# Two softmax maps of a second attention layer joined by GpSimd before their transposes, quads unrolled

## The chip, the cores and the metric

The kernel runs on one core of a Trainium2 chip. The metric is the device time of one launch in microseconds (us), as the median of the runs shown. The profile is of one execution.

## The reference, cut to what matters

A two-layer transformer tower over 32 images of 37 tokens, width 192, 12 heads of 16. The layer-1 attention is the part that changes:

```python
q = (x @ Wq).reshape(B, N, 2, H, D).transpose(2, 0, 3, 1, 4)   # two sets of queries
k = (x @ Wk).reshape(B, N, 2, H, D).transpose(2, 0, 3, 1, 4)   # and of keys
v = (x @ Wv).reshape(B, N, H, D).transpose(0, 2, 1, 3)
out = softmax(q[0] k[0]^T / 4) v - exp(lambda_p) * softmax(q[1] k[1]^T / 4) v
h = layernorm(h + out @ Wo + bo)
```

Before it stand a patch embedding, a layer-0 attention and a mixture of 64 slots (its output is combined and normalized here, as h); behind it an expert layer with top-4 gates and a last norm.

## The kernel before, in words

Every engine has one queue of instructions written by hand, and semaphores order them: TensorE (pe), VectorE (dve), ScalarE (act), GpSimd (pool) and the DMA queue (sp). One stage follows the other: layer 0 (to 231 us), the slots' matmuls, bound by the weights' DMA (to 423 us), the stage that changes (`l1_pe`, `l1_dve`, `l1_act`, `l1_pool`, L867 to L1026, 423 to 634 us), the top-4 gates (to 718 us), the expert units (to 977 us), and the last norm.

The 32 images are 16 pairs, two images in partitions 0 to 36 and 64 to 100 (101 rows, `ROWS`). Four pairs are a quad, and there are four quads. `steps` (L861) writes out quads 0 and 3 and makes quads 1 and 2 a loop. In a quad (`step`, L889):

- `combine` (L868) makes the slots' output of a pair (L871), VectorE adds h1 (L926) and takes the norm's moments (`ln_moments`, L571, L574), GpSimd makes the reciprocal root (`pool_rstd`, L584, L586), and VectorE scales (`ln_scale`, L579) into `h_in`.
- `pe_turn` transposes `h_in` (L334), `take_turned` copies it (L344). `pe_qk` (L353) makes queries and keys in blocks of 96 rows, two for each map: 16 products of 296 columns. ScalarE copies queries (L442), and ScalarE (L447) and VectorE (L457) write each key block six times, masked for one head each. `pe_v` (L370) makes the values, `dve_v` (L474) takes them.
- `pe_attention` (L420) goes over 8 units, a pair and a map each. A unit's scores (L388) are 444 columns in one bank; VectorE takes the maximum and subtracts it (L480, L485), ScalarE takes the exponential (L490), TensorE makes 6 transposes (L399), ScalarE copies them (L497), TensorE mixes with the values and a column of ones (L415, 12 small products), and `dve_norm` (L520 to L533) divides by the row sums, weights the second map with lambda and subtracts it. TensorE's queue runs two units ahead of the mixing.
- `pe_turn_rows` (L552), `take_rows` (L560), the projection (L905), the residual (L961), its moments, GpSimd's root, `ln_scale`, the transposes for the expert layer (L880, L979), and GpSimd's `h3_all` (L1011).

Map 0 of the next quad's queries and keys is made at the end of a quad, map 1 only after the residual. At the start GpSimd also writes ones into `zs` (L1020), which waits only for the first root:

```python
pool.wait_ge(L0["rstd"], QUADS + 1)
pool.memset(zs[6 * SR:ZR, :, :], 1.0).then_inc(s_set, 1)
```

## Time and profile before

| what | value |
|---|---|
| median of 3 runs | 1006.28 us (1004.51 to 1006.57) |
| the profiled execution, its own time | 1001.23 us |
| its span | 999.4 us |
| granted TensorE clock, mean | 0.854 |
| TensorE, VectorE, ScalarE, GpSimd busy | 794.8, 562.6, 368.2, 106.6 us |

Busy time is that of the whole span, over stages with different limits; a stage is read from its own windows and its own timeline. A line of a timeline can hold several instructions (x6), and its duration is then from the first start to the last end. A bracket says how long the engine had been idle, and what ended that.

### The profile page before, as it was taken

Reading aid. Unit: us, or ns where it says so; the run is one execution under the profiler, and the core shown is the slowest. Engines: PE = TensorE matmul, PEld = TensorE weight load, DVE = VectorE, ACT = ScalarE, POOL = GpSimd, SP = SyncE. Lnnn points to the kernel's source line nnn. Section 1 sums busy time; section 2 is a strip of 40 time slices with the busy share of each in tenths; the row PEclk is TensorE's granted clock in tenths of the full one; section 3 lists DMA queues with packets and bytes.
Section 4 is the critical chain, followed back from the end, with each engine's and each line's share of the span. In section 5 each row is a group of like instructions: output and inputs, shape, how many; then the busy total and the mean of one; then the engine's idle time right before and its main releaser. Section 6 shows DMA issues by size and latency. Waiting matters only on the chain.

```text
span 999.4 us, 19725 instructions
## 1 busy us (share of the span) xinstructions
PE 794.8 (80%) x6898; PEld 452.0 (45%) x6898; DVE 562.6 (56%) x1562; ACT 368.2 (37%) x785; POOL 106.6 (11%) x134
## 2 busy tenths in 40 slices
PE   6889899839888687529988988634399989989992
PEld 4567676635434343216766666311133333333331
DVE  4565664640110111155686859588687858848785
ACT  0313221303211210004333444143387767758770
POOL 0020202022121200030010010132200000000002
PEclk9898987957976979758798979855599999989996
DMA  8510100003999999993000000362300000000001
GB/s 301 225 38 1 36 0 0 1 1 139 416 424 424 415 414 427 279 123 45 1 2 1 0 1 2 121 73 49 86 13 2 2 2 1 0 2 1 0 1 38
DMA packets 25016, 102.56 MB, mean 103 GB/s; under 512 B 3552, under 2 KB 14756, under 8 KB 20724
## 3 DMA queue, kind: packets, MB, share of 16 engines
q1 hardware_dynamic: 23894, 98.37, 29.2%
q0 software_dynamic: 1056, 3.44, 0.9%
q8 instruction: 27, 0.44, 0.2%
q14 instruction: 39, 0.31, 0.1%
HBM read 93.08 MB, written 5.07 MB: 98 GB/s over the span
## 4 chain that ended last, share of the span: by engine, by line
PE 60%; DVE 17%; DMA 11%; issue 6%; POOL 2%; ACT 2%; DVEq 0%; POOLq 0%; SPq 0%; ACTq 0%
DMA stream<-in_fc_dram 10%; PE P L1461 8%; PE P L1436 7%; PE P L1445 7%; PE P L353 6%; PE P L769 3%; PE P L388 3%; PE P L415 3%; PE P L370 2%; PE P L399 2%; DVE work L579 2%; PE P L1454 2%; PE P L738 2%; PE P L744 2%; PE P L1179 2%
## 5 line engine op out<-in xcount | busy, mean ns | idle before, releaser
L1603 DVE TENSOR_TENSOR work<-work,P 128x396 f32<-128x396 f32 x384 | 193.1, 562 | 65.1 <-PE P L1445 45.0
L1532 ACT ACTIVATE work<-P 128x396 f32<-128x396 f32 x384 | 178.6, 500 | 56.9 <-PE P L1436 55.8
L1436 PE MATMUL P<-stream 99*128 x384 | 129.5, 340 | 12.3 <-ACT work L1532 10.5
L1445 PE MATMUL P<-early,middle 96*128 x384 | 129.8, 339 | 0.6 <-DVE work L1603 0.6
L1461 PE MATMUL P<-work 128*32 128x396 f32 x768 | 84.6, 508 | 0.0
L1436 PEld LDWEIGHTS P<-stream 99*128 99x128 bf16 x384 | 37.7, 98 | 100.6 <-ACT work L1532 54.2
L584 POOL TENSOR_SCALAR work<-work 101x4 f32<-101x4 f32 x16 | 3.7, 230 | 652.8 <-DVE work L574 652.8
L796 ACT ACTIVATE work<-P 128x768 f32<-128x768 f32 x16 | 13.0, 812 | 153.8 <-PE P L751 153.8
L811 DVE COPY work<-P 128x768 f32<-128x768 f32 x16 | 15.3, 958 | 96.0 <-PE P L759 96.0
L490 ACT ACTIVATE work<-work 101x444 f32<-101x444 f32 x48 | 28.1, 585 | 85.9 <-DVE work L485 85.9
L1106 PE MATMUL P<-early 128*37 128x192 f32 x384 | 47.8, 337 | 10.1 <-DMA early<-in_patches_dram 7.1
L1445 PEld LDWEIGHTS P<-early,middle 96*128 96x128 bf16 x384 | 37.8, 98 | 35.3 <-DVE work L1603 17.4
L816 DVE COPY work<-P 128x192 f32<-128x192 f32 x16 | 5.7, 358 | 79.0 <-PE P L769 79.0
L769 PE MATMUL P<-stream,work 128*32 128x192 f32 x768 | 46.0, 403 | 3.2 <-DVE work L811 3.2
L415 PE MATMUL P<-work 101*37 101x34 f32 x1152 | 46.0, 209 | 2.8 <-DVE work L474 2.8
L399 PE MATMUL P<-ident,work 101*128 101x101 f32 x288 | 36.3, 264 | 12.6 <-ACT work L490 10.6
L415 PEld LDWEIGHTS P<-work 101*37 101x37 f32 x1152 | 41.5, 123 | 8.1 <-issue 3.9
L1106 PEld LDWEIGHTS P<-early 128*37 128x37 f32 x384 | 34.4, 117 | 22.4 <-issue 10.4
L353 PE MATMUL P<-work,stream 96*96 96x296 f32 x128 | 41.3, 487 | 4.1 <-DVE work L961 3.5
L480 DVE TENSOR_REDUCE work<-P 101x12 f32<-101x444 f32 x48 | 29.6, 616 | 22.5 <-PE P L388 22.2
L457 DVE TENSOR_SCALAR stream<-P,hmask 96x296 f32<-96x296 f32 x48 | 21.5, 515 | 36.8 <-PE P L353 36.8
L399 PEld LDWEIGHTS P<-ident,work 101*128 101x128 f32 x288 | 27.4, 144 | 29.7 <-ACT work L490 19.4
(212 smaller groups left out, 1247.6 us busy)
## 6 DMA issues: line engine op xcount, KB each, us to landing
stream<-in_fc_dram SPq DMA_DIRECT2D x16, 2304.0 KB
stream<-in_fc_dram SPq DMA_DIRECT2D x16, 1536.0 KB, 17.5
stream<-in_fc_dram SPq DMA_DIRECT2D x16, 768.0 KB, 19.1
early<-stream SPq DMA_DIRECT2D x36, 99.0 KB, 2.3
early<-in_patches_dram SPq DMA_DIRECT2D x4, 888.0 KB, 5.1
stream<-w_dram SPq DMA_DIRECT2D x6, 512.0 KB
work<-in_w_dram SPq DMA_DIRECT2D x1, 2048.0 KB, 8.3
stream<-z_dram SPq DMA_DIRECT2D x6, 297.0 KB, 10.3
```

The costliest lines, as they stand in the source:

```text
L353: mm = pe.matmul(P[0:FH, at + mc, 0:QT], w[:, kc, m * D + mc * FH:m * D + (mc + 1) * FH], h_t[:, kc, :, :], start=(kc == 0), stop=(kc == 1))
L388: mm = pe.matmul(P[64 * e:64 * e + T, u % 2, mc * HH * T:(mc + 1) * HH * T], q_t[:, m, mc, b * T:(b + 1) * T], k_heads[:, m, mc, b, :, :], ...
L399: mm = pe.transpose(P[:, 4 + 2 * (u % 2) + hp // 3, (hp % 3) * ROWS:(hp % 3 + 1) * ROWS], probs[0:ROWS, u % 2, hp, :, :].rearrange("p a k ...
L415: mm = pe.matmul(P[64 * e:64 * e + T, 2 + u % 2, hp * w2:(hp + 1) * w2], probs_t[0:ROWS, u % 2, hp, 64 * e:64 * e + T], v_blk[0:ROWS, 2 * ...
L480: dve.tensor_reduce(row_max[0:ROWS, u % 2, :], src, AX, ALU.max).then_inc(L["row_max"], 1)
L769: mm = pe.matmul(P[32 * j:32 * j + B, 6 + u, 0:D], hidden_t[:, u, c, B * j:B * (j + 1)], fc2[:, u, c, j, :], start=False, stop=(c == HC - ...
L1106: mm = pe.matmul(P[64 * e:64 * e + T, 2 + j // 2, (j % 2) * D:(j % 2 + 1) * D], patches[:, c, 2 * j + e, :], w_patch[:, c, :], start=(c == ...
L1436: pe.matmul(P[:, n % 3, 0:TC], w1s[:, seg, i * 128:(i + 1) * 128], zs[:, seg, ds(it * TC, TC)], start=True, stop=True).then_inc(s_u1, 1)
L1445: pe.matmul(P[:, 3 + n % 3, 0:TC], gate_sel[:, c, :], ws[:, 2 * seg + hh, ds(it * TC, TC)], start=True, stop=True).then_inc(s_bc, 1)
L1461: pe.matmul(P[32 * j:32 * j + 32, 6 + sq, 0:TC], w2[:, i, seg, :], gated[:, n % 8, :], start=False, stop=(hh == 1 and c == CH // 2 - 1), s ...
L1532: act.activation(act_out[:, n % 4, :], P[:, n % 3, 0:TC], ACT.Gelu_apprx_tanh).then_inc(s_ua, 1)
L1603: dve.tensor_tensor(gated[:, n % 8, :], act_out[:, n % 4, :], P[:, 3 + n % 3, 0:TC], ALU.mult).then_inc(s_ug, 1)
```

## The change

It touches only the stage of layer 1, and where its four weight matrices lie and are loaded. All four quads are written out. Queries and keys come in three blocks of 128 rows (8 heads; the middle block holds 4 heads of each map), 12 products of 296 columns, and a key block is written eight times: blocks 0 and 2 by ScalarE, block 1 by VectorE. A step is now a pair with both maps: its scores fill two banks (888 columns), VectorE takes maximum, difference, sums and reciprocals over 24 head rows, ScalarE the exponential in place, and GpSimd multiplies both maps with their weights (`differ`) and subtracts them. One set of 6 transposes and 12 mixing products follows, without the column of ones, and ScalarE copies the result (`take_mixed`). The residual's norm goes to GpSimd (`normed`), with h plus bias (`with_bias`). The parts of neighbouring quads are put between the pairs. The memset of `zs` now waits for `with_bias(0)`.

```diff
-k_heads1 = tenant(stream, FH, 12 * D, [2, 2, QB, HH, T])
+k_heads1 = tenant(stream, 128, 0, [3, QB, 8, T])
...
-late = Tenants(stream)
+late = Tenants(early)
...
+exps = [shifted, w([128, 2, NH, T])]
+res = w([128, QP, D])
...
+hb = rowc[:, 0:QP, :]
+q_t1 = tenant(work, 128, shared + 2 * QB * H_STRIDE, [3, QT])
...
+    sp.wait_ge(s_emb, QP * QUADS)
+    sp.wait_ge(s_prep_misc, PREP_MISC)
+    for dst, name in ((w_q1, "w_q1"), (w_k1, "w_k1"), (w_v1, "w_v1"), (w_o1, "w_o1")):
+        sp.dma_start(dst, io[name]).then_inc(s_late, 16)
...
-    for dst, name in ((w_q1, "w_q1"), (w_k1, "w_k1"), (w_v1, "w_v1"), (w_o1, "w_o1")):
-        sp.dma_start(dst, io[name]).then_inc(s_late, 16)
...
+    def combine(q):
+        if q:
+            pe.wait_ge(L1["taken"], QP * (q - 1) + 1)
         for j in range(QP):
...
+            mm = pe.matmul(P[0:ROWS, 4 + j // 2, (j % 2) * D:(j % 2 + 1) * D], combine_all[:, q * QP + j, :],
+                           y2[:, q * QP + j, :], start=True, stop=True, skip_group_check=True)
...
+    def turn_in(q):
+        if q:
+            pe.wait_ge(L1["taken"], QP * (q - 1) + 2)
...
+    def turn_x3(q):
+        pe.wait_ge(L1["shifted"], min(QP * (q + 1) + 2, QP * QUADS))
...
+    def qk(q, n):
+        if n == 0:
+            pe.wait_ge(L1["h_t"], QP * (q + 1))
+        if n < 2 and q:
+            pe.wait_ge(L1["shifted"], QP * q - 1 + n)
+        if n == 2:
+            pe.wait_ge(L1["q_ready"], 3 * q + 1)
+            pe.wait_ge(L1["k_ready_a"], 2 * HB * q + HB)
+        for w, bank, made in ((w_q1, 2 * (n % 2), "q_made"), (w_k1, 2 * (n % 2) + 1, "k_made")):
             for kc in range(2):
...
+                mm = pe.matmul(P[:, bank, 0:QT], w[:, kc, n * 128:(n + 1) * 128], h_t[:, kc, :, 0:T],
+                               start=(kc == 0), stop=(kc == 1))
...
+    def scores(q, p):
+        g = QP * q + p
+        if p == 0:
+            pe.wait_ge(L1["q_ready"], 3 * (q + 1))
+            pe.wait_ge(L1["k_ready_a"], 2 * HB * (q + 1))
+            pe.wait_ge(L1["k_ready_v"], HB * (q + 1))
+        if p >= 2:
+            pe.wait_ge(L1["shifted"], g - 1)
+        if p == 3 and q:
+            pe.wait_ge(LO["h_t"], QP + QP * q)
+        for m in range(2):
+            for e in range(2):
+                b = 2 * p + e
+                for n, h, to, at in ((2 * m, 0, HB, 4 * T * m), (1, 4 * m, 4 * m + 4, HB * T * (1 - m))):
+                    mm = pe.matmul(P[64 * e:64 * e + T, 2 * (g % 2) + m, at:at + (to - h) * T],
+                                   q_t1[:, n, b * T:(b + 1) * T], k_heads1[:, n, b, h:to, :],
+                                   start=True, stop=True, skip_group_check=True)
...
+    def turn_probs(q, p):
+        g = QP * q + p
+        if g >= 2:
+            pe.wait_ge(L1["taken"], g - 1)
+        if p == 0:
+            pe.wait_ge(L1["v_ready"], 4 * (q + 1))
+        elif p == 1 and q:
+            pe.wait_ge(LO["resid"], QP * q)
+        elif p == 2 and q + 1 < QUADS:
+            pe.wait_ge(L0["resid"], QP * (QUADS + q + 2))
+        elif p == 3 and q + 1 < QUADS:
+            pe.wait_ge(L1["h_t"], QP * (q + 2))
+        elif p == 1:
+            pe.wait_ge(L1["h_t"], QP)
+        pe.wait_ge(L1["mapped"], g + 1)
...
+    combine(0)
+    turn_in(0)
+    for n in range(3):
+        qk(0, n)
+    values(0)
+    for q in range(QUADS):
+        more = q + 1 < QUADS
+        scores(q, 0)
+        scores(q, 1)
+        if q:
+            project(q - 1)
+        scores(q, 2)
+        turn_probs(q, 0)
+        mix(q, 0)
+        turn_probs(q, 1)
+        if more:
+            combine(q + 1)
+        if q:
+            turn_x3(q - 1)
+        scores(q, 3)
+        mix(q, 1)
+        turn_probs(q, 2)
+        if more:
+            turn_in(q + 1)
+        mix(q, 2)
+        if more:
+            qk(q + 1, 0)
+        turn_probs(q, 3)
+        if more:
+            qk(q + 1, 1)
+        mix(q, 3)
+        if more:
+            values(q + 1)
+            qk(q + 1, 2)
+        turn_attn(q)
+    project(QUADS - 1)
     turn_x3(QUADS - 1)
...
+    def softmax(q, p):
+        g = QP * q + p
+        src = P[0:ROWS, 2 * (g % 2):2 * (g % 2) + 2, 0:NH * T].rearrange("p m (h k) -> p m h k", k=T)
+        dve.wait_ge(L1["scores"], g + 1)
+        dve.tensor_reduce(row_max1[0:ROWS, g % 2, :, :], src, AX, ALU.max).then_inc(L1["row_max"], 1)
+        dve.wait_ge(L1["row_max"], g + 1)
+        if g >= 2:
+            dve.wait_ge(L1["mapped"], g - 1)
+        dve.tensor_tensor(exps[g % 2][0:ROWS], src, spread(row_max1[0:ROWS, g % 2, :, :], 3, T),
+                          ALU.subtract).then_inc(L1["shifted"], 1)
+    def weights(q, p):
+        g = QP * q + p
+        dve.wait_ge(L1["exps"], g + 1)
+        dve.tensor_reduce(sums[0:ROWS, g % 2, :, :], exps[g % 2][0:ROWS], AX, ALU.add).then_inc(L1["sums"], 1)
+        dve.wait_ge(L1["sums"], 3 * g + 1)
+        dve.reciprocal(shares[0:ROWS, g % 2, :, :], sums[0:ROWS, g % 2, :, :]).then_inc(L1["sums"], 1)
+        dve.wait_ge(L1["sums"], 3 * g + 2)
+        dve.tensor_tensor(shares[0:ROWS, g % 2, 1, :], shares[0:ROWS, g % 2, 1, :], lam[0:ROWS, :],
+                          ALU.mult).then_inc(L1["sums"], 1)
...
+    def residual(q):
+        dve.wait_ge(s_hb, q + 1)
+        if q:
+            dve.wait_ge(LO["h_out"], QP * q)
...
+    combined(0)
+    normed(0)
+    take_in(0)
+    dve.wait_ge(s_hm, 1)
+    keys(0, 1)
+    values(0)
+    for q in range(QUADS):
+        more = q + 1 < QUADS
+        softmax(q, 0)
+        weights(q, 0)
+        softmax(q, 1)
+        if q:
+            residual(q - 1)
+        weights(q, 1)
+        softmax(q, 2)
+        if more:
+            combined(q + 1)
+        if q:
+            take_out(q - 1)
+        weights(q, 2)
+        if more:
+            normed(q + 1)
+        softmax(q, 3)
+        if more:
+            take_in(q + 1)
+        weights(q, 3)
+        if more:
+            keys(q + 1, 1)
+            values(q + 1)
+    residual(QUADS - 1)
...
+    take_in(0)
+    act.wait_ge(s_hm, 1)
+    queries(0, 0)
+    keys(0, 0)
+    queries(0, 1)
+    queries(0, 2)
+    keys(0, 2)
+    for q in range(QUADS):
+        more = q + 1 < QUADS
+        exp(q, 0)
+        exp(q, 1)
+        take_probs(q, 0)
+        exp(q, 2)
+        take_mixed(q, 0)
+        take_probs(q, 1)
+        if q:
+            take_out(q - 1)
+        exp(q, 3)
+        take_mixed(q, 1)
+        take_probs(q, 2)
+        if more:
+            take_in(q + 1)
+        take_mixed(q, 2)
+        if more:
+            queries(q + 1, 0)
+            keys(q + 1, 0)
+        take_probs(q, 3)
+        if more:
+            queries(q + 1, 1)
+        take_mixed(q, 3)
+        if more:
+            queries(q + 1, 2)
+            keys(q + 1, 2)
+        take_rows(act, q, s_at, s_att, 6)
+    take_out(QUADS - 1)
...
+    def differ(q, p):
+        g = QP * q + p
+        pool.wait_ge(L1["sums"], 3 * (g + 1))
+        pool.tensor_tensor(exps[g % 2][0:ROWS], exps[g % 2][0:ROWS], spread(shares[0:ROWS, g % 2, :, :], 3, T),
+                           ALU.mult).then_inc(L1["weighted"], 1)
+        pool.wait_ge(L1["weighted"], g + 1)
+        if g >= 2:
+            pool.wait_ge(L1["probs_turned"], g - 1)
+        e = exps[g % 2][0:ROWS].rearrange("p m (h a) k -> p m h a k", a=2)
+        pool.tensor_tensor(probs[0:ROWS, g % 2, :, :, 0:T], e[:, 0], e[:, 1], ALU.subtract).then_inc(L1["mapped"], 1)
...
+    def normed(q):
+        settle(pool, LO["mv"], QP * q + QP)
+        pool.tensor_scalar(var_o[0:ROWS, :], mv_o[0:ROWS, :, 1], EPS, None, ALU.add).then_inc(LO["var"], 1)
+        pool.wait_ge(LO["var"], q + 1)
+        pool.tensor_tensor(rstd_o[0:ROWS, :], var_o[0:ROWS, :], negh[0:ROWS, :], ALU.pow).then_inc(LO["rstd"], 1)
+        pool.wait_ge(LO["rstd"], q + 1)
+        if q:
+            pool.wait_ge(LO["h_turned"], 2 * q)
+        for j in range(QP):
+            pool.tensor_scalar(h_out[0:ROWS, j, :], res[0:ROWS, j, :], mv_o[0:ROWS, j, 0:1],
+                               rstd_o[0:ROWS, j:j + 1], ALU.subtract, ALU.mult).then_inc(LO["h_out"], 1)
...
+    with_bias(0)
     pool.wait_ge(s_fo, GROUPS)
-    pool.wait_ge(L0["rstd"], QUADS + 1)
+    pool.wait_ge(s_hb, 1)
     pool.memset(zs[6 * SR:ZR, :, :], 1.0).then_inc(s_set, 1)
     pool.wait_ge(s_set, 1)
-    steps(pool, step)
+    for q in range(QUADS):
+        differ(q, 0)
+        if q:
+            normed(q - 1)
+        differ(q, 1)
+        if q:
+            keep(q - 1)
+            with_bias(q)
+        if q + 1 < QUADS:
+            pool_rstd(pool, L0, QUADS + q + 1)
+        differ(q, 2)
+        differ(q, 3)
+    normed(QUADS - 1)
+    keep(QUADS - 1)
...
```

## Rows read from the trace of the kernel before

**Rows 1.** Windows: engines' busy time in one quad; first line names the columns.

```profile
core 0: us, PE busy (x) PEld busy (x) DVE busy (x) ACT busy (x) POOL busy (x), PEclk, DMA share, GB/s
498.00:543.00 45.00, 40.14 (x449) 29.99 (x448) 33.51 (x99) 17.40 (x38) 4.82 (x6) 0.92 0.01 1
```

**Rows 2.** Timeline (start us, us, engine, line): scores of quads 0, 2, 3; end.

```profile
462.77 1.52 PE L388 MATMUL P<-stream,work 96*37 96x222 f32 x14
...
554.17 0.96 PE L388 MATMUL P<-stream,work 96*37 96x222 f32 x8
...
600.95 0.95 PE L388 MATMUL P<-stream,work 96*37 96x222 f32 x8
...
633.42 0.53 DVE L979 COPY early<-P 96x148 f32<-96x148 f32 x2 [0.71 <-PE P L880]
```

**Rows 3.** Timeline at the start of the stage.

```profile
431.46 3.06 PE L871 MATMUL P<-early 128*101 128x192 f32 x8 [8.19 <-issue]
...
437.90 9.38 DVE L579 TENSOR_SCALAR work<-work 101x192 f32<-101x192 f32 x4 [1.62 <-POOL work L586]
437.99 8.01 POOL L1020 MEMSET stream<- 3x9504 bf16 x1
```

**Rows 4.** Timeline of quad 2: one instance of each TensorE piece.

```profile
547.08 4.22 PE L353 MATMUL P<-work,stream 96*96 96x296 f32 x16 [1.19 <-DVE work L961]
...
551.23 2.87 PE L370 MATMUL P<-stream,work 96*37 96x96 f32 x64
...
559.08 0.74 PE L399 MATMUL P<-ident,work 101*128 101x101 f32 x6
...
563.43 0.93 PE L415 MATMUL P<-work 101*37 101x34 f32 x24
```

**Rows 5.** The same timeline: one instance of each VectorE piece.

```profile
545.93 1.01 DVE L961 TENSOR_TENSOR work<-P,work 101x384 f32<-101x384 f32 x2
...
553.95 1.23 DVE L579 TENSOR_SCALAR work<-work 101x192 f32<-101x192 f32 x4
...
562.57 0.23 DVE L522 RECIPROCAL work<-work 101x12 f32<-101x12 f32 x1
...
563.11 0.61 DVE L480 TENSOR_REDUCE work<-P 101x12 f32<-101x444 f32 x1
...
563.75 0.62 DVE L485 TENSOR_TENSOR work<-P,work 101x444 f32<-101x444 f32 x1
...
565.74 0.17 DVE L525 TENSOR_TENSOR work<-work,lam 101x12 f32<-101x12 f32 x1
...
576.90 0.95 DVE L942 TENSOR_TENSOR work<-work,rowc 101x768 f32<-101x768 f32 x1
```

**Rows 6.** The same timeline: ScalarE's and GpSimd's pieces.

```profile
548.83 1.04 POOL L586 TENSOR_TENSOR work<-work,negh 101x4 f32<-101x4 f32 x1
...
550.34 2.48 ACT L447 ACTIVATE stream<-P,hmask 96x296 f32<-96x296 f32 x6 [0.58 <-PE P L353]
...
555.37 1.81 POOL L1011 TENSOR_TENSOR h_all<-work,rowc 101x768 f32 x1 [5.50 <-DVE work L579]
...
564.41 0.59 ACT L490 ACTIVATE work<-work 101x444 f32<-101x444 f32 x1 [1.53 <-DVE work L485]
...
564.89 0.65 ACT L497 ACTIVATE work<-P 128x606 f32<-128x606 f32 x1
```

**Rows 7.** Timeline after the stage: small VectorE product alone, then beside GpSimd.

```profile
660.73 0.18 DVE L1571 TENSOR_TENSOR work<-work 128x32 f32<-128x32 f32 x1
...
663.74 1.06 POOL L1612 TENSOR_TENSOR work<-work 128x512 f32<-128x512 f32 x1 [1.91 <-DVE work L1567]
663.78 1.06 DVE L1571 TENSOR_TENSOR work<-work 128x32 f32<-128x32 f32 x1
```

**Rows 8.** Timeline before quad 1: TensorE at its lower clock.

```profile
485.58 1.27 PE L399 MATMUL P<-ident,work 101*128 101x101 f32 x6 [1.66 <-ACT work L490]
...
492.01 6.03 PE L353 MATMUL P<-work,stream 96*96 96x296 f32 x16
```

More of the change, by code:

```diff
@@ L316, in tower @@
         s_yt = sem("s_slot_inputs_taken")
-        s_keep = sem("s_h1_kept")
         SMALL_LOADS = [
@@ L975, in take_x3 @@
-        def take_x3(eng, copy, quad, g):
-            eng.wait_ge(LO["h_turned"], nth(quad, 2, g + 1))
-            src = P[0:FH, 4 + g, :].rearrange("p (j k e r) -> p j k e r", j=2, k=2, e=2)
-            for j in range(2):
-                copy(x3_t[:, :, ds(quad * QB + (4 * g + 2 * j), 2), :], src[:, j, :, :, 0:T]).then_inc(LO["h_t"], 1)
-        def l1_act(act):
-            def step(it, first, last):
-                act_q(act, L1, it, 2, (1,), None, k_heads1)
-                act_attention(act, L1, it, 2, None if first else lambda: take_x3(act, act.copy, it - 1, 0))
-                if not last:
-                    take_turned(act, act.copy, L1, it + 1, 0, h_t)
-                take_rows(act, it, s_at, s_att, 6)
-                if not last:
-                    act_q(act, L1, it + 1, 2, (0,), None, k_heads1)
-            act.activation(lam[:, :], lam[:, :], ACT.Exp).then_inc(s_lam, 1)
-            take_turned(act, act.copy, L1, 0, 0, h_t)
-            act_q(act, L1, 0, 2, (0,), None, k_heads1)
-            steps(act, step)
-            take_x3(act, act.copy, QUADS - 1, 0)
@@ L997, in l1_pool @@
-        def l1_pool(pool):
-            def stage(quad):
-                pool.tensor_copy(comb_r[:, :, :], combine_all[:, ds(quad * QP, QP), :]).then_inc(s_cr, 1)
-            def step(it, first, last):
-                if not last:
-                    pool.wait_ge(s_mix, nth(it, QP, QP))
-                    stage(it + 1)
-                    pool_rstd(pool, L0, it + (QUADS + 1))
-                pool_rstd(pool, LO, it)
-                pool.wait_ge(LO["h_out"], nth(it, QP, QP))
-                pool.tensor_tensor(h3_all[0:ROWS, ds(it * QP, QP), :], h_out[0:ROWS, :, :],
-                                   spread(rowc[0:ROWS, 5, :], 1, QP), ALU.add).then_inc(s_h3, 1)
+            combine(0)
@@ new lines, in l1_pe, with take_h, take_x3 @@
+            project(QUADS - 1)
+            turn_x3(QUADS - 1)
+        def take_h(copy, q, g):
+            src = P[0:FH, 6 + g, :].rearrange("p (j k e r) -> p j k e r", j=2, k=2, e=2)
+            for j in range(2):
+                copy(h_t[:, :, 4 * g + 2 * j:4 * g + 2 * j + 2, 0:T], src[:, j, :, :, 0:T]).then_inc(L1["h_t"], 1)
+        def take_x3(copy, q, g):
+            src = P[0:FH, 2 + g, :].rearrange("p (j k e r) -> p j k e r", j=2, k=2, e=2)
+            for j in range(2):
+                at = q * QB + 4 * g + 2 * j
+                copy(x3_t[:, :, at:at + 2, :], src[:, j, :, :, 0:T]).then_inc(LO["h_t"], 1)
```

265 lines of the change are left out of this document (170 added, 95 removed).

## The prediction

> **What bounds the kernel now.** I read the busy slices first: the stage of layer 1 is the only one the change touches. Its windows come next: in a middle quad TensorE is busy 40 of 45 us, VectorE 33.5, GpSimd 5 [rows 1]. Then the timeline for the quads' beginnings: first scores at 462.8, 554.2 and 600.9, the end at 634.0 [rows 2]. So quads 0 and 1 together take 91.4, quad 2 takes 46.8, quad 3 has nothing to prepare and takes 33.0: 171.1 in all. Inside a quad, eight units follow one another every 2.9 us while two are in flight, and some 20 us go to the handover, where TensorE and VectorE take turns. At the start one thing stands out: four scalings that take 1.23 elsewhere [rows 5] take 9.38 beside GpSimd's memset of 8.0 [rows 3].
>
> **Durations, each for one step.** TensorE [rows 4]: scores of a pair 1.9 (the same 1776 columns as two units of 0.96 [rows 2]); transposes 0.75; mixing 0.9; a block's queries and keys, 8 instructions of L353, 2.1; values 2.9; combine of four pairs 1.8 (at most the 3.1 of [rows 3], which has waits in it); eight transposes 1.5, the nearest row being L399's six in 0.74 to 1.27 [rows 4, 8].
>
> VectorE [rows 5]: 444 columns take 0.61 and 768 take 0.95, so 888 take 1.07: maximum and subtraction together 2.2; sums 1.07, reciprocal of 24 (12 take 0.23) 0.3, lambda 0.17: weights 1.6. Residual or combine's sum, 1.0, and its moments 1.4: 2.4 (GpSimd's root starts at 548.83, 2.9 after L961, with 0.5 of its own ahead). Scaling 1.25. A pair of copies 0.55.
>
> ScalarE [rows 6]: exponential of 888 between 0.59 (444 columns) and twice that; 0.95, since a part is fixed. Copy of transposes 0.65, mixed result 0.35 (estimate), a key block 8 x 0.41 = 3.3.
>
> GpSimd has no such product in the trace. 512 elements take 1.06 [rows 7], 768 take 1.81 [rows 6]. The bounds for 888 are 1.06 and 2.1; it has more elements than either row, so I take 1.95, and 1.0 for the difference of 444. With 0.3 to be released, a map step takes 3.25; from 1.9 to 3.5 is possible. The residual's norm: root 1.6 (1.04 is the power [rows 6]) and four scalings of 192 at about 0.4: 3.3.
>
> The Trainium skill's GPSIMD Engine Reference (Engine selection) advises against just this: elementwise work with two inputs is put at about twice VectorE's time. By that the product would take 2.15 and the difference 1.25, and the sum below would be some 3.5 us longer. My sum goes by the rows, which are GpSimd's own.
>
> **A middle quad after the change**, from the issue of its first scores. Scores 1.9, maximum and subtraction to 4.15, exponential to 5.15, weights to 6.8, second softmax to 9.05, residual of the quad before to 11.65, second weights to 13.3. GpSimd finished map 0 at 10.15, but takes the residual's norm before map 1: 11.65 to 14.9. Map 1 is ready at 18.1. TensorE has mixed pair 0 by 12.6 and its next instruction is the transpose of map 1: it stands for 5.5 us, with combine, the old quad's transposes and the last scores queued behind. Then transposes 18.9, combine 20.7, VectorE's half sum and moments to 22.7 (it had been idle since 15.5), copy and third weights to 24.9. Scaling 26.2, last softmax 28.4, exponential 29.4, copy of pair 1's result (behind it in ScalarE's queue) 29.8, transposes of h 31.3, copies 31.9, and only now the last weights, 33.5. Map 3 is ready at 36.8, transposed 37.6, block 1's products 39.7, mixing 40.7, values 43.5, block 2's products 45.6, ScalarE's eight key copies 49.0. Period **49.0**, against 46.8.
>
> The other two by the same walk. Quad 0 has no residual, norm or h3 in it: map 1 at 15.15, combine's sum 19.9, third weights 21.5, last weights 30.2, map 3 33.6, next scores at **45.7**. Quad 3 prepares nothing, but its tail is serial: last weights at 27.2, map 3 30.6, transposes, copy, mixing, copy 33.4, transposes of rows 34.8, projection's start 35, residual to 40.4, norm on GpSimd 43.6, transposes and copies **44.6** (33.0 before). Together 45.7 + 2 x 49.0 + 44.6 = 188.3, against 171.1: +17.2.
>
> **The start.** The memset now follows the scalings: they take 1.25, not 9.38, -8.1. From there to the first scores I count 14.9 in place of 15.5 (8 fewer instructions of L353, but block 2 waits for ScalarE's block 0, then 3.3 of key copies): -8.8 in all. The memset runs beside products and copies out of PSUM and is over 5 us before the first scores; the first map step comes 7 us later. If that cover were gone it would cost up to 8.
>
> **Shared access.** A VectorE product of 0.18 took 1.06 beside a GpSimd product of 1.06, and a scaling waited 8 us for the memset [rows 7, 3]. Here `normed(q+1)`, four scalings out of SBUF, starts 0.2 before GpSimd's map 2. One scaling gets through; the others wait for the product, perhaps the difference: 2.1 to 3.1. I take 2.5 in each of three quads: +7.5. The lambda products fall where GpSimd is idle or in short steps: 0, or 2 each if they don't.
>
> **The clock.** After a sparse stretch TensorE was at its lower level: six transposes took 1.27 for 0.74, and sixteen of L353 6.03 for 4.22 although it worked without a break [rows 8, 4]. An idle of 5.5 us in each quad invites that. On the path of a middle quad: two sets of transposes +1.0, combine +0.5, block 1 +0.9, mixing and scores +0.6: +3.0; for quads 0 and 3 +2.0. In all **+10**, between 0 and 27 (the lower level for the whole path: 6 to 7 a quad).
>
> **At nothing:** the weights' four loads go ahead of the slots' stream, past nothing that runs; before, they were issued behind its last load. The staging copy of combine and the column of ones were beside other work. Writing out the loop: quads in it and outside it took alike. Merged semaphores change no order.
>
> **Sum:** +17.2 - 8.8 + 7.5 + 10 = +26, less 1 for the pieces where a lower clock and a blocked scaling overlap: +25. The profiled execution took 1001.2, 5 below the median of 1006.3; the stage is all of the change, so I put the +25 on the median: **1031**.
>
> **Rivals.**
> - *Bare waits* (0.13). Neither sharing nor clock costs: VectorE's scalings slip through before GpSimd asks, and products back to back keep the clock up. +8.4: 1015.
> - *GpSimd is quick* (0.20, the other side). If a map step takes 2.0, as its copies would suggest, map 1 comes 1.25 sooner and the norm's scalings 1.0, map 3 1.25, and the two waits in between shorten: 4.4 in quads 1 to 3, 2.5 in quad 0, 15.7 in all, and TensorE's idle shrinks to 3 us; at best neither clock nor sharing then costs anything. +8.4 - 15.7 = -7: 999. It decides from a map step under 2.6. For it: engine work in a middle quad is only some 32 on TensorE and 29 on VectorE, so there is room below 46 down to 985. Against it: 512 elements already take 1.06 [rows 7], and 768 take 1.81 [rows 6].
> - *The lower clock stays* (0.12). TensorE's work falls from 40 [rows 1] to 32 in 50 us, in bursts. +8.4 + 7.5 + 27: 1049.
> - *Ends meet* (0.05): errors of both signs cancel at 1006.
>
> **Numbers.** The forecast, 1018 to 1043, has 0.50. About 0.2% is what a measurement of this kernel can tell from no change. Faster comes from the quick GpSimd alone: 0.20. Same: 0.05. Slower: the rest, 0.75. The range of 8 in 10 goes from 1003, leaving out most of the quick case, to 1046, leaving out most of the slow clock.
>
> **What would show it.** Right: first scores near 454; quads near 48, 54, 54, 48 apart; a wait of TensorE's transposes for GpSimd's difference of 2 to 6 us once a quad; VectorE waiting for combine some 4 us; one `ln_scale` instruction of 2 us a quad; a product on GpSimd of 1.9 to 2.1; mean clock in the stage under 0.8. Wrong: a product under 1.3, quads under 44, or TensorE without such gaps.

## The result, and the profile after

The changed kernel takes **1046.96 us** in the median of four runs (1040.55, 1042.09, 1051.84, 1053.09) against 1006.42 for the kernel before. The ratio of the two means is 1.0382, 95% interval 1.0279 to 1.0485. The runs of either kernel fall into two groups some 11 us apart (before: 1001 to 1008 and 1014 to 1023), and this median lies between the two. The profiled execution is the fastest of the four, 1040.55 for a span of 1038.7; the one of before took 1001.2.

The page of the changed kernel, its first and second part in extract:

```profile
span 1038.7 us, 18375 instructions
...
PE 789.4 (76%) x6386; PEld 450.8 (43%) x6386; DVE 533.5 (51%) x1407; ACT 364.4 (35%) x781; POOL 172.2 (17%) x182
```

Three engines have less work than before, and GpSimd, with 66 us more, is busy 17% of the span: no engine became the bound, and yet the span is longer. Where the quads begin and end, from the timeline of TensorE and of VectorE (start, us, engine, line; L883 is combine, L959 the scores, L1068 the last copy of the turned rows):

```profile
436.04 2.85 PE L883 MATMUL P<-early,combine_all 128*101 128x192 f32 x8 [8.23 <-DMA early<-y_dram]
...
458.65 1.58 PE L959 MATMUL P<-stream,work 128*37 128x296 f32 x14 [0.64 <-issue]
...
507.74 4.66 PE L959 MATMUL P<-stream,work 128*37 128x296 f32 x32 [2.74 <-issue]
...
563.78 3.21 PE L959 MATMUL P<-stream,work 128*37 128x296 f32 x32 [2.74 <-issue]
...
618.35 3.21 PE L959 MATMUL P<-stream,work 128*37 128x296 f32 x32 [2.74 <-issue]
...
671.61 0.53 DVE L1068 COPY early<-P 96x148 f32<-96x148 f32 x2 [6.30 <-PE P L891]
```

And the windows from scores to scores (us, then the busy time of TensorE, its weight loads, VectorE, ScalarE and GpSimd, then the granted clock, the DMA share and GB/s):

```profile
458.65:507.74 49.09, 32.01 (x296) 24.75 (x297) 27.13 (x49) 15.57 (x34) 12.47 (x10) 0.79 0.10 13
507.74:563.78 56.04, 37.37 (x321) 28.73 (x322) 29.14 (x60) 16.68 (x38) 21.30 (x18) 0.73 0.01 1
563.78:618.35 54.57, 35.92 (x320) 28.14 (x321) 29.14 (x60) 16.67 (x38) 21.29 (x18) 0.75 0.00 1
618.35:672.14 53.79, 31.07 (x240) 23.78 (x240) 20.32 (x45) 9.97 (x20) 26.32 (x23) 0.61 0.00 1
```

From the first combine to the first scores it is 22.6 us, 31.3 before [rows 2, 3]. The four quads take 213.5, 171.1 before. The stage is 236.1 against 202.5: +33.6. Of the +39.3 between the two profiled executions, 4.6 lie ahead of the stage and 1.1 behind it, where the code is that of before.

One wait shows how a quad got long. Quad 1, the timeline of GpSimd, TensorE and VectorE (L1270 product, L1277 difference, L1289 the residual's scalings, L983 transposes of the maps, L883 the next quad's combine):

```profile
517.61 1.13 POOL L1277 TENSOR_TENSOR work<-work 101x444 f32<-101x444 f32 x1
...
521.83 3.99 POOL L1289 TENSOR_SCALAR work<-early 101x192 f32<-101x192 f32 x4
525.79 1.67 POOL L1270 TENSOR_TENSOR early<-early 101x888 f32<-101x888 f32 x1
527.54 1.12 POOL L1277 TENSOR_TENSOR work<-early 101x444 f32<-101x444 f32 x1
...
528.81 1.25 PE L983 MATMUL P<-ident,work 101*128 101x101 f32 x6 [7.35 <-POOL work L1277]
529.85 2.77 PE L883 MATMUL P<-early,combine_all 128*101 128x192 f32 x8
...
531.48 0.56 DVE L1103 TENSOR_TENSOR work<-P,h_all 101x384 f32<-101x384 f32 x1 [7.68 <-PE P L883]
```

The weights of map 1 (the map of the quad's second pair; pairs count from 0) were there at 521.7. GpSimd was on the residual's norm until 525.8, TensorE stood 7.35 us, and VectorE 7.68 us for a combine that needed nothing from map 1. The table of waits adds them up over the stage (us in all, times, longest):

```profile
PE P L983 <- POOL work L1277: 42.3, 12, 7.4
DVE work L1103 <- PE P L883: 31.0, 8, 9.3
```

The next quad's four scalings on VectorE (L589), beside GpSimd's product of map 2:

```profile
536.51 3.52 DVE L589 TENSOR_SCALAR work<-work 101x192 f32<-101x192 f32 x4
536.67 1.75 POOL L1270 TENSOR_TENSOR work<-work,early 101x888 f32<-101x888 f32 x1 [0.47 <-DVE early L1095]
```

GpSimd's rows of the stage, against which the prediction's estimates stand, and VectorE's scalings (the groups by form; busy us, mean ns):

```profile
L1289 POOL TENSOR_SCALAR work<-early 101x192 f32<-101x192 f32 x16 | 15.9, 1006 | 0.4
...
L1270 POOL TENSOR_TENSOR early<-early 101x888 f32<-101x888 f32 x8 | 13.4, 1676 | 28.4 <-DVE early L1095 28.4
L1277 POOL TENSOR_TENSOR work<-work 101x444 f32<-101x444 f32 x8 | 9.0, 1125 | 0.6
...
L589 DVE TENSOR_SCALAR work<-work 101x192 f32<-101x192 f32 x16 | 11.8, 796 | 1.9 <-POOL work L596 1.9
```

### The profile page after: what moved, and what is told of

Read it like the earlier page. It is cut to its first block, busy times and chain, and to the rows that moved or that the text cites. A ratio compares the mean times of both kernels' runs of the same rounds, so it can differ in the third digit from the quotient of the medians.

```text
span 1038.7 us, 18375 instructions
## 1 busy us (share of the span) xinstructions
PE 789.4 (76%) x6386; PEld 450.8 (43%) x6386; DVE 533.5 (51%) x1407; ACT 364.4 (35%) x781; POOL 172.2 (17%) x182
## 4 chain that ended last, share of the span: by engine, by line
PE 55%; DVE 17%; DMA 10%; issue 7%; POOL 6%; ACT 4%; POOLq 0%; SPq 0%; DVEq 0%; ACTq 0%
DMA stream<-in_fc_dram 9%; PE P L1765 8%; PE P L1740 7%; PE P L1749 7%; PE P L782 3%; PE P L925 2%; PE P L363 2%; DVE work L589 2%; PE P L1483 2%; PE P L1758 2%; DVE work L1880 2%; PE P L751 2%; POOL work L1289 2%; PE P L398 1%; PE P L757 1%
## 5 line engine op out<-in xcount | busy, mean ns | idle before, releaser
L782 PE MATMUL P<-stream,work 128*32 128x192 f32 x768 | 48.2, 417 | 3.2 <-DVE work L824 3.2
L983 PE MATMUL P<-ident,work 101*128 101x101 f32 x96 | 16.6, 332 | 42.3 <-POOL work L1277 42.3
L1410 PEld LDWEIGHTS P<-early 128*37 128x37 f32 x384 | 34.6, 118 | 22.8 <-issue 10.5
L959 PE MATMUL P<-stream,work 128*37 128x296 f32 (+1 forms) x256 | 32.3, 407 | 12.9 <-issue 8.9
L1715 PE MATMUL P<-ident,work 128*128 128x128 f32 x40 | 11.2, 434 | 36.5 <-DVE work L1894 36.5
L925 PE MATMUL P<-work,early 96*128 96x296 f32 x96 | 35.8, 532 | 2.1 <-ACT stream L1225 1.5
L782 PEld LDWEIGHTS P<-stream,work 128*32 128x32 f32 x768 | 28.7, 136 | 19.4 <-DVE work L824 5.0
L777 PE MATMUL P<-fc_b,slot_sel 4*128 4x192 f32 x32 | 11.5, 445 | 30.3 <-DMA stream<-in_fc_dram 30.3
L983 PEld LDWEIGHTS P<-ident,work 101*128 101x128 f32 x96 | 13.3, 191 | 45.7 <-issue 45.3
L751 PE MATMUL P<-stream,slot_sel 4*128 4x384 f32 x64 | 31.2, 615 | 0.0
```

What stands on the lines that cost most here:

```text
L751: pe.matmul(P[:, 2 * u + n, 0:HID // 2], slot_sel[:, :], fc1_b[:, u, n * (HID // 2):(n + 1) * (HID // 2)], start=True, stop=False, skip_gr ...
L782: mm = pe.matmul(P[32 * j:32 * j + B, 6 + u, 0:D], hidden_t[:, u, c, B * j:B * (j + 1)], fc2[:, u, c, j, :], start=False, stop=(c == HC - ...
L925: mm = pe.matmul(P[:, bank, 0:QT], w[:, kc, n * 128:(n + 1) * 128], h_t[:, kc, :, 0:T], start=(kc == 0), stop=(kc == 1))
L959: mm = pe.matmul(P[64 * e:64 * e + T, 2 * (g % 2) + m, at:at + (to - h) * T], q_t1[:, n, b * T:(b + 1) * T], k_heads1[:, n, b, h:to, :], s ...
L983: mm = pe.transpose(P[:, pair_bank(g) + hp // 3, (hp % 3) * ROWS:(hp % 3 + 1) * ROWS], probs[0:ROWS, g % 2, hp, :, :].rearrange("p a k -> ...
L1410: mm = pe.matmul(P[64 * e:64 * e + T, 2 + j // 2, (j % 2) * D:(j % 2 + 1) * D], patches[:, c, 2 * j + e, :], w_patch[:, c, :], start=(c == ...
```

## The experiments

Twelve kernels, each with one profiled execution; two were timed in five rounds. Times in us; q0 to q3 are the periods from the first scores of a quad to those of the next (q3: to the last copy of the turned rows), stage is from the first combine to that copy. "Time" is that of the profiled execution.

| kernel | first combine | to scores | q0 | q1 | q2 | q3 | stage | time |
|---|---|---|---|---|---|---|---|---|
| before | 431.5 | 31.3 | 91.4 for both | | 46.8 | 33.0 | 202.5 | 1001.2 |
| after | 436.0 | 22.6 | 49.1 | 56.0 | 54.6 | 53.8 | 236.1 | 1040.6 |
| e1 | 436.9 | 22.7 | 49.2 | 53.2 | 54.6 | 53.7 | 233.4 | 1036.9 |
| e2 | 440.2 | 23.4 | 48.5 | 52.0 | 53.0 | 53.7 | 230.6 | 1039.2 |
| e3 | 437.5 | 22.7 | 47.7 | 54.5 | 54.6 | 55.1 | 234.6 | 1040.5 |
| e6 | 448.9 | 22.6 | 49.1 | 51.7 | 52.1 | 46.4 | 221.8 | 1036.8 |
| e5 | 438.7 | 22.5 | 49.0 | 53.9 | 54.2 | 54.1 | 233.7 | 1039.5 |
| e7 | 448.2 | 22.5 | 49.0 | 56.0 | 54.6 | 53.8 | 235.9 | 1052.5 |
| b1 | 437.0 | 23.3 | 91.4 for both | | 46.8 | 33.0 | 194.6 | 998.8 |
| x1 | 437.1 | 22.7 | 37.9 | 38.6 | 46.7 | 42.9 | 188.8 | 992.7 |
| x2 | 437.0 | 22.8 | 32.6 | 34.2 | 34.1 | 42.9 | 166.6 | 972.1 |
| x3 | 436.5 | 23.0 | 39.3 | 39.6 | 40.6 | 47.3 | 189.7 | 992.5 |
| x4 | 437.1 | 22.8 | 41.2 | 40.9 | 41.0 | 43.4 | 189.3 | 993.8 |
| x5 | 431.2 | 23.0 | 32.6 | 34.2 | 34.0 | 43.1 | 166.9 | 966.8 |

**One part of these periods is no edit's.** The first scores of a quad take 3.21 us at the upper level of TensorE's clock and 4.6 or more where they begin at the lower one, behind the same idle time of 2.74. In the changed kernel q1 has the one and q2 the other, and the first transposes come 11.15 and 9.68 us after the first scores:

```profile
518.89 0.71 PE L983 MATMUL P<-ident,work 101*128 101x101 f32 x6 [2.05 <-POOL work L1277]
...
573.46 0.71 PE L983 MATMUL P<-ident,work 101*128 101x101 f32 x6 [2.04 <-POOL work L1277]
```

That is the whole difference between q1 and q2. In the experiments on the changed kernel it falls on other quads. e1, q2:

```profile
561.96 4.64 PE L959 MATMUL P<-stream,work 128*37 128x296 f32 x32 [2.75 <-issue]
...
573.07 0.71 PE L983 MATMUL P<-ident,work 101*128 101x101 f32 x6 [2.04 <-POOL work L1277]
```

So here are the periods less what the first transposes came later than 9.68 us (9.74 in q0), called "at equal first scores" below:

| kernel | q0 | q1 | q2 | q3 | four quads against the changed kernel |
|---|---|---|---|---|---|
| after | 49.1 | 54.6 | 54.6 | 53.8 | |
| e1 | 49.2 | 53.2 | 53.2 | 52.3 | -4.3 |
| e2 | 48.5 | 51.5 | 51.6 | 53.7 | -6.7 |
| e3 | 47.7 | 53.0 | 53.1 | 53.6 | -4.6 |
| e6 | 49.1 | 50.2 | 50.6 | 46.4 | -15.8 |
| e5 | 49.0 | 52.5 | 52.8 | 53.2 | -4.6 |
| e7 | 49.0 | 54.6 | 54.6 | 53.8 | -0.1 |

**e1: map 1 ahead of the residual's norm** (GpSimd's queue)

```diff
     differ(q, 0)
+    differ(q, 1)
     if q:
         normed(q - 1)
-    differ(q, 1)
```

> GpSimd makes pair 1's maps before it takes the residual's norm; nothing else moves. In the changed kernel the norm stands 5.3 us ahead of them (root 1.3, four scalings 1.0 each) in quads 1 to 3. Theory 'a serial chain of hand-overs': the wait of TensorE's transposes for pair 1's maps falls from 7.4 to about 3.4 us, but the old quad's h_out, GpSimd's two additions and the next root then come later, so that a middle quad gains only 1 to 2 us and quad 3 about 3: stage 236 -> 230. Rival 'the transposes' wait is what counts': 4 us in each of three quads, stage 224. Rival 'other work hides it': no change.

The stage falls by 2.7. At equal first scores it is 1.4 to 1.5 in each of the three quads that the edit touches, 4.3 in all, near the 1 to 2 of the theory (3 were expected in q3). TensorE's wait for map 1 falls from 7.4 to 3.3, but the norm now comes later, and with it the old quad's transposes ahead of the last scores; the wait for map 2 rises from 0.8 to 2.8 in q1 and q2. The next wait in the row takes most of it.

**e2: combine ahead of the transposes of map 1** (TensorE's queue)

```diff
+    if more:
+        combine(q + 1)
     turn_probs(q, 1)
-    if more:
-        combine(q + 1)
```

> TensorE's queue: combine(q+1) goes ahead of the transposes of pair 1. VectorE waits 7.7 us for it in a middle quad. Theory 'queue order': that wait goes, but the transposes for the expert layer and the copies still stand behind pair 1's maps, so the third weights come 2.5 to 3 us sooner: about 7 us over quads 0 to 2, stage 229. Rival 'GpSimd's maps end everything': no change (within 1 us). Rival 'the whole wait of VectorE returns': 18 to 20 us.

-5.5, and at equal first scores -6.7: 0.6 in q0, 3.1 in q1 and 2.9 in q2, as the theory had it (2.5 to 3 in each of three quads), but for q0. VectorE starts on the next quad's moments sooner, but its norm is still behind the third weights.

**e3: the next quad's norm alone, not beside the product**

```diff
     if q + 1 < QUADS:
         pool_rstd(pool, L0, QUADS + q + 1)
+        pool.wait_ge(L0["h_out"], QP * (QUADS + q + 2))
     differ(q, 2)
```

> GpSimd waits for the four scalings of normed(q+1) before it starts the product of map 2, so that the two don't run at once. In the changed kernel the scalings take 3.5 us instead of 1.25. Theory 'shared access': the last softmax comes 2.3 us sooner in quads 0 to 2, stage 236 -> 229; GpSimd's third maps come 1.2 later, which TensorE covers. Rival 'GpSimd's delay counts': gain under 3 us in all, or a loss of up to 3.

The four scalings take 1.25 again in every quad, so the 2.3 us of shared access are real (VectorE's longest single one is 0.38, 1.74 in the changed kernel):

```profile
536.74 1.25 DVE L589 TENSOR_SCALAR work<-work 101x192 f32<-101x192 f32 x4
...
538.07 1.68 POOL L1270 TENSOR_TENSOR work<-work,early 101x888 f32<-101x888 f32 x1 [1.64 <-DVE work L589]
```

The stage falls by 1.5 only. At equal first scores q0, q1 and q2 lose 1.4 to 1.6 each, 4.6 with a little in q3; the first scores of q2 and q3, at the lower level in this execution (4.77 and 4.79 for 3.21), took 3.0 of that back. So some 1.5 of the 2.3 lie on the path, with GpSimd's map 2 coming later by the edit itself.

**e6: the residual's four scalings back on VectorE**, behind the third softmax

```diff
-    for j in range(QP):
-        pool.tensor_scalar(h_out[0:ROWS, j, :], res[0:ROWS, j, :], mv_o[0:ROWS, j, 0:1],
-                           rstd_o[0:ROWS, j:j + 1], ALU.subtract, ALU.mult).then_inc(LO["h_out"], 1)
...
     softmax(q, 2)
+    if q:
+        scaled(q - 1)
```

> The residual's four scalings (4 x 1.0 us on GpSimd) go to VectorE (1.25 in all), behind its third softmax; the root stays on GpSimd. Theory 'the scalings are the mis-sized term': pair 1's maps come 4 us sooner in quads 1 to 3, and after the last quad another 2.7: stage 236 -> about 222. Rival 'VectorE pays it back': 4 us at the end of quad 3 only, stage 232.

The last quad's scalings go to VectorE too. -14.3, as expected; at equal first scores -15.8: 4.3, 4.0 and 7.4 in q1 to q3, most in q3, where the norm stands once ahead of map 1 and once in the serial tail. No other single edit to the changed kernel gives as much. The windows of q1 and q3:

```profile
520.63:572.30 51.67, 37.03 (x320) 28.70 (x321) 30.98 (x64) 16.70 (x38) 17.39 (x14) 0.76 0.00 1
...
624.36:670.72 46.36, 28.56 (x240) 22.72 (x240) 23.41 (x53) 9.97 (x20) 18.63 (x15) 0.70 0.00 1
```

**e5: TensorE kept at work while it waits for map 1**

```diff
+    if q and p == 1:
+        for _ in range(16):
+            pe.matmul(P[:, pair_bank(g), 0:128], ident[:, :], ident[:, :], start=True, stop=True)
     pe.wait_ge(L1["mapped"], g + 1)
```

> The changed kernel with 16 more 128x128 matmuls in quads 1 to 3 while TensorE waits for the second pair's maps (their result is overwritten by the transposes). Theory (TensorE falls to the lower clock because it waits there, and what follows the wait pays): the second set of transposes takes 0.71 instead of 1.25 us, the combine 1.4 to 1.5 instead of 2.77, the first queries and keys 2.26 instead of 4.32; a middle quad loses about 5 us, the stage 10 to 12. Rival (the low clock is bought back by nothing so short, or lies beside other waits): each quad changes by under 2 us.

The clock comes up, and the instructions behind the wait get short, the combine 1.47 for 2.77 (timeline of TensorE):

```profile
531.10 0.74 PE L986 MATMUL P<-ident,work 101*128 101x101 f32 x6 [2.11 <-POOL work L1280]
531.68 1.47 PE L883 MATMUL P<-early,combine_all 128*101 128x192 f32 x8
```

The windows of its two middle quads:

```profile
510.15:564.09 53.94, 38.41 (x352) 30.85 (x353) 29.25 (x60) 16.69 (x38) 21.34 (x18) 0.85 0.00 1
564.09:618.25 54.16, 38.57 (x352) 31.14 (x353) 29.24 (x60) 16.70 (x38) 21.34 (x18) 0.84 0.00 1
```

The granted clock is 0.85 and 0.84 for 0.73 and 0.75, yet the stage falls by 2.4, far from the 10 to 12 of the theory. At equal first scores it is 2.1, 1.8 and 0.6 in q1 to q3; the first scores of q2 and q3 at the lower level took 2.4 back. The queries and keys at the quad's end still run at the lower level too (4.09 for eight, 2.26 elsewhere), so this edit does not price the whole clock. Part of what it saves turns into waiting: the transposes of map 2 now wait 2.16, 0.77 before. The result is nearer the rival's under 2 us a quad.

**e7: the weights' loads at the old place**

```diff
-    sp.wait_ge(s_emb, QP * QUADS)
-    sp.wait_ge(s_prep_misc, PREP_MISC)
-    for dst, name in ((w_q1, "w_q1"), (w_k1, "w_k1"), (w_v1, "w_v1"), (w_o1, "w_o1")):
-        sp.dma_start(dst, io[name]).then_inc(s_late, 16)
...
     sp.wait_ge(s_hid, GROUPS - 1)
+    for dst, name in ((w_q1, "w_q1"), (w_k1, "w_k1"), (w_v1, "w_v1"), (w_o1, "w_o1")):
+        sp.dma_start(dst, io[name]).then_inc(s_late, 16)
```

> The changed kernel with the four weight loads of the second layer where the kernel before has them, behind the last slots' hidden rows. Theory (the first combine is 4.6 us later because the first layer ran at a lower granted clock, not because of where the loads stand): the first combine comes at 436 to 440 us again, total about 1040. Rival (the loads at 160 us hold up the first layer or the slots' weights): the first combine comes at about 431.5 us, total about 1036.

The first combine comes at 448.2, later still, so the early loads don't explain the 4.6 us ahead of the stage. The four periods are those of the changed kernel to 0.1 us. What moved is layer 0, which had a lower clock in this execution (0.86 and 0.79 in its first two 100 us, 0.91 and 0.85 in the changed kernel's, 0.93 and 0.87 before).

**b1: the kernel before with one part of the change alone**, the memset behind the first norm's scalings

```diff
-            pool.wait_ge(L0["rstd"], QUADS + 1)
+            pool.wait_ge(L0["h_out"], QP * (QUADS + 1))
             pool.memset(zs[6 * SR:ZR, :, :], 1.0).then_inc(s_set, 1)
```

> The kernel before with one part of the change alone: GpSimd's memset of three partitions stands behind the first norm's scaling instead of ahead of it. Theory (the start's gain of the change is this memset alone): VectorE's four scalings, 9.38 us there, take about 1.25, the first scores come 8.1 us after the first combine sooner, the total is 1006.3 - 8.1 = 998. Rival (GpSimd's memset then holds up something else of VectorE, the copies of the turned rows or of the keys): the gain is under 3 us, the total over 1003.

The timeline of VectorE, GpSimd and TensorE:

```profile
443.48 1.25 DVE L579 TENSOR_SCALAR work<-work 101x192 f32<-101x192 f32 x4 [1.62 <-POOL work L586]
...
444.85 8.01 POOL L1020 MEMSET stream<- 3x9504 bf16 x1 [1.41 <-DVE work L579]
...
460.34 1.71 PE L388 MATMUL P<-stream,work 96*37 96x222 f32 x16
```

998.73 in the median of 6 runs, ratio to before 0.9879, 95% interval 0.9819 to 0.9939. Combine to scores takes 23.3 for 31.3, and nothing else in the stage moves. This one wait is 8.0 of the change's gain of 8.7 at the start.

**x1: the layout kept, the order rewritten**

TensorE's queue as it is afterwards, in extract; a + marks what stands at a new place, and the old places are left out:

```diff
     scores(q, 1)
+    if q:
+        turn_attn(q - 1)
+    if more:
+        combine(q + 1)
     scores(q, 2)
+    if q:
+        project(q - 1)
     turn_probs(q, 0)
+    if q >= 2:
+        turn_x3(q - 2)
     scores(q, 3)
     mix(q, 0)
     turn_probs(q, 1)
+    if more:
+        turn_in(q + 1)
...
```

with VectorE, ScalarE and GpSimd to match: `combined(q + 1)` behind the second softmax, the next norm behind the second weights, the residual's scalings on VectorE, input and bias summed into the quad's own rows of `h1_all` (the single buffer `hb` would have held the next norm back), and the turned input in banks 0 and 1.

> The changed kernel's block layout and GpSimd's join kept, the order rewritten: the next quad's combine right behind the first scores, its norm by the second weights, the residual's scalings on VectorE, the turned input in the score banks 0 and 1, the rows of a quad turned for the MLP two quads later, the attention's rows turned in the next quad, the sum of input and bias in the rows of h1 (no second buffer). Theory (the quads are long because of the order of the waits, not because of GpSimd's durations or the layout): a period of 38 to 43 us instead of 53 to 56, the stage 185 to 200 us, total 990 to 1005. Rival (GpSimd's 2.9 us for each pair and the lower clock set the period whatever the order): periods stay at 48 or more, the total over 1020.

Periods of 38 to 39 in q0 and q1, a stage of 188.8, as the theory had it. In q2 a new wait shows: TensorE's last scores stand behind a copy that VectorE does after a norm, which in turn is slowed by the product beside it.

```profile
549.80 3.51 DVE L588 TENSOR_SCALAR work<-work 101x192 f32<-101x192 f32 x4
549.97 1.75 POOL L1297 TENSOR_TENSOR early<-early 101x888 f32<-101x888 f32 x1 [1.12 <-DVE early L1094]
...
553.24 0.52 DVE L1067 COPY early<-P 96x148 f32<-96x148 f32 x2
...
553.90 3.19 PE L960 MATMUL P<-stream,work 128*37 128x296 f32 x16 [6.30 <-DVE early L1067]
```

**x2: those waits taken out**

```diff
-    if q:
-        residual(q - 1)
     weights(q, 1)
-    if more:
-        normed(q + 1)
     if q >= 2:
         take_out(q - 2)
+    if q:
+        residual(q - 1)
     softmax(q, 2)
+    if more:
+        normed(q + 1)
...
     keys(q + 1, 1)
+    keys(q + 1, 2)
```

The last line is block 2's keys, on VectorE now and no longer on ScalarE. TensorE makes block 2's products and the last transposes ahead of the third mixing, and from quad 2 on the first mixing comes ahead of the last scores.

> The reordered version with three more moves: VectorE's half of the turned rows of two quads ago copied right behind the second weights (TensorE waited 6.3 us for it in the third quad), the next quad's norm behind the third softmax instead of beside GpSimd's product (3.51 us there, 1.25 alone), and the keys of the third chunk on VectorE, with the third queries and keys ahead of the third mixing. Theory (each period is a chain of waits that still has slack in it): periods of 35 to 37 us, the third no longer than the second, the stage 172 to 180 us, total 975 to 985. Rival (VectorE, busy 31 us of 38 before and 34 now, sets the period): periods of 38 to 40, total 985 to 990.

**971.86** in the median of 6 runs, ratio to before 0.9643, 95% interval 0.9575 to 0.9711: the fastest of the kernels timed in rounds, and faster than both. The first three periods lie 1 to 2 us under the theory's 35 to 37, and the stage, 166.6, is 5 below its range. The moves were made together, so their shares aren't known. The four quads in the windows:

```profile
459.76:492.38 32.62, 25.43 (x288) 19.14 (x290) 29.02 (x58) 12.18 (x25) 14.29 (x11) 0.95 0.14 18
492.38:526.60 34.22, 31.47 (x317) 25.84 (x314) 30.96 (x70) 13.31 (x27) 17.29 (x14) 0.85 0.01 2
526.60:560.67 34.07, 28.67 (x325) 22.91 (x322) 32.49 (x74) 13.29 (x29) 17.31 (x14) 1.00 0.01 1
560.67:603.61 42.94, 29.05 (x263) 23.96 (x257) 25.01 (x58) 10.66 (x22) 16.83 (x14) 0.76 0.00 1
```

In q2 VectorE is busy 32.5 of 34.1 us (the third busy time), and the clock is at its upper level all through: with the waits gone it came up by itself.

**x3: x2 with the join on VectorE**

```diff
     weights(q, 0)
+    differ(q, 0)
     softmax(q, 1)
...
-    pool.tensor_tensor(exps[g % 2][0:ROWS], exps[g % 2][0:ROWS], spread(shares[0:ROWS, g % 2, :, :], 3, T),
-                       ALU.mult).then_inc(L1["weighted"], 1)
+    dve.tensor_tensor(exps[g % 2][0:ROWS], exps[g % 2][0:ROWS], spread(shares[0:ROWS, g % 2, :, :], 3, T),
+                      ALU.mult).then_inc(L1["weighted"], 1)
...
```

> The same kernel as the run before it, but with the join of the two maps (product of 888, difference of 444 elements) on VectorE right behind the weights. Theory (in this order GpSimd's join is cover for VectorE and is worth keeping): VectorE gets 4 x (0.95 + 0.5) = 6 us more in each quad, on top of 34, and the period grows by 3 to 6 us, the total by 10 to 20. Rival (GpSimd's 2.9 us and its two extra hand-overs in each pair's chain cost more than 1.5 us on VectorE): the period stays or shrinks, the total within 3 us of the run before it or below.

VectorE does a join in 1.08 + 0.62 where GpSimd takes 1.68 + 1.12, and yet the total is 20 us longer, at the upper end of what was expected. The groups by form, and the window of q2:

```profile
L1105 DVE TENSOR_TENSOR work<-work,early 101x888 f32<-101x888 f32 x4 | 4.3, 1082 | 0.1
...
L1112 DVE TENSOR_TENSOR work<-work 101x444 f32<-101x444 f32 x4 | 2.5, 622 | 0.1
```

```profile
538.31:578.86 40.55, 32.88 (x326) 25.98 (x322) 38.69 (x82) 13.52 (x29) 6.12 (x6) 0.83 0.00 1
```

VectorE is given 6.8 us a quad, the periods grow by 4.3 to 6.7, and VectorE is busy 38.7 of 40.6 in q2. So in this order the idea of the change is sound: the slower engine is the right one for the join. In the changed kernel's own order that wasn't tried.

**x4: x2 with the combine at the change's place**

```diff
     scores(q, 1)
     if q:
         turn_attn(q - 1)
-    if more:
-        combine(q + 1)
...
     turn_probs(q, 1)
+    if more:
+        combine(q + 1)
```

with its sum and moments behind the third softmax and its norm behind the third weights.

> The fastest reordered version with one thing put back as the change has it: the next quad's combine behind the second set of transposes, its sum and moments behind the third softmax, its norm behind the third weights. Theory (the late combine alone makes a quad long, since the next quad's norm, transposes, queries, keys and first scores stand in one row behind it): the first three periods grow from 34 to 40 or 43, the fourth stays at 43, the total is 990 to 998. Rival (the other moves, the scalings, the second place of the turned rows and the keys on two engines, made the gain): periods grow by under 2 us, the total stays under 978.

+22.7 on the stage, 6.7 to 8.6 in each quad that prepares another, +0.5 in the one that doesn't: the theory's numbers.

**x5: the four scalings on GpSimd, at the queue's end**

```diff
     differ(q, 3)
+    if 0 < q < QUADS - 1:
+        scaled(q - 1)
     if q:
         keep(q - 1)
```

> The fastest reordered version with the residual's four scalings back on GpSimd in the second and third quad, but behind the last join of the quad instead of ahead of the second one. Theory (their 4 us cost the change time only because the next join and its transposes stand behind them): no period grows by over 0.5 us, the total stays within 3 us of 970, or 1 to 3 us below. Rival (4 us more of GpSimd's work in a quad cost time wherever they stand, by the lock on the shared access or by the next quad's first join): two periods grow by 2 us or more each.

It concerns q1 and q2; the scalings of q3 and of the tail stay on VectorE. The scalings of q2 in GpSimd's timeline, and the window of that quad:

```profile
549.44 4.00 POOL L1323 TENSOR_SCALAR work<-early 101x192 f32<-101x192 f32 x4
```

```profile
520.95:554.99 34.04, 28.54 (x325) 22.99 (x322) 30.96 (x70) 13.31 (x29) 21.00 (x18) 1.00 0.01 1
```

The same 4.0 us of GpSimd work in q1 and q2, worth 4.3 and 4.0 in e6, cost nothing here. They save nothing either: the stage is 166.9 for 166.6, and the 966.8 comes from an earlier first combine (431.2 for 437.0). The total of 1 to 3 us less that the expectation allowed didn't come from this edit, so 1.5 us less on VectorE in a quad don't shorten it: it isn't bound by VectorE alone.

## Why the prediction was right in direction and short in size

**The start** was right: -8.8 predicted (its terms, 8.1 and 0.6, add up to 8.7), 31.3 to 22.6 measured, and b1 shows that the memset is 8.0 of it, against the 8.1 taken.

**The mechanism of the quads** was right. The wait at map 1 was named and sized at 5.5 before sharing and clock; it is 7.35. VectorE's wait for combine (some 4 us) is 7.68. Of the signs named, the clock of the stage is there (0.72, under 0.8); the product of 1.9 to 2.1 is not, it takes 1.68.

**The sizes.** With its penalties, the prediction's periods were 50.2, 54.5, 54.5 and 46.6, less 1; measured 49.1, 56.0, 54.6 and 53.8. Nearly all of the miss is q3: 7.2 of 8.7 us.
- *GpSimd's scalings* are the mis-sized term. Four at about 0.4 were taken, estimated without a row of such an operation on GpSimd; they take 1.006 each, 3.98 for four. That is 2.3 us more each time they stand on the path: once in q1 and q2, twice in q3 (ahead of map 1 and in the tail), so 4.6 of q3's 7.2. e6 takes them from the path: 4.3, 4.0 and 7.4 at equal first scores, where 4.0 ahead of map 1 in each quad, and 4.0 less VectorE's 1.25 in the tail, make 14.7.
- *The clock in q3's tail*: 2.0 was taken for the quad. The projection alone takes 5.44 there for 2.85, and the granted clock of the quad is 0.61, against 0.73 to 0.79 in the others:

```profile
512.34 2.85 PE L1014 MATMUL P<-early,work 96*101 96x192 f32 x16
...
657.83 5.44 PE L1014 MATMUL P<-early,work 96*101 96x192 f32 x16
```

- *Product and difference*: 1.95 and 1.0 taken, 1.68 and 1.12 measured. Their sum, 2.8 for 2.95, was good. The Trainium skill's GPSIMD Engine Reference (Engine selection) puts elementwise work with two inputs at about twice VectorE's time: here it is less, 1.55 times for the product (1.68 by 1.08, x3) and 1.8 for the difference (1.12 by 0.62). For the scalings it is more, 3.2 times: four take 3.98 on GpSimd and 1.25 on VectorE.
- *Shared access*: 2.5 in each of three quads was taken for the next norm beside the product; the scalings take 3.52 for 1.25, 2.3 more. Right as a duration; on the path it is some 1.5 (e3 at equal first scores), so the term was 1.0 too high in each.
- *The clock in the middle quads*: +3.0 taken, and the sum fits. What is shown is 2.1 and 1.8 by e5, and another 1.5 in q1 for the first scores, which q2 was spared; the queries and keys at the lower level (4.32 for 2.26) were not priced. With the scalings 2.3 too low and the shared access 1.0 too high, the right total for q1 and q2 is partly luck, and what made good the rest is open.

**At nothing:** the weights' loads were put at nothing, and e7 bears that out. Ahead of the stage 4.6 us came that no term had. They belong to the execution, not to the change: b1, whose code up to the stage is that of before, has its first combine at 437.0 too. x5, with the loads at their new place, has it at 431.2. So +33.6 of the +39.3 is the change's, in the stage, against +25 forecast; for the 1.1 behind it no run shows a cause. The median, 1046.96, is further from 1031 and just above the range's 1046; the ratio of the means, 1.0382, is inside it (1044.7). The 0.2% that the prediction put as what a measurement can tell was too fine: the interval is 1% to either side.

**The rivals.** "GpSimd is quick" fell: a map step takes 2.8 and its release. "The lower clock stays" (1049) came near in number, but its mechanism isn't shown: the granted clock was 0.73 to 0.79 in three of the quads, above the lower level, and with the clock partly held up by e5 the stage loses 2.4 of the 33.6 (4.6 at equal first scores). What the lower level costs in all is open. What no rival had is that the order, not any duration, was worth most: x2, with the same layout and the same join, has a stage 69.5 us shorter than the changed kernel. The place of the combine, with the chain behind it, is worth 22.7 in x2 (x4). How the rest splits between the scalings, the queries' and keys' waits and the rows of the old quad was not taken apart further. In the new order the join on GpSimd is no loss: without it x2's stage is 23.1 longer (x3), 189.7, only 4.9 below that of b1, the kernel before with its memset moved. Whether it costs or saves in the changed kernel's order no run shows.
